# Tile-by-tile routing, folded queries on three bank pairs, sums by four heads, and a residual added by an identity product, in a two-layer perceiver kernel

## The reference

```python
    x = x + _L0_xattn_ref(_layernorm(x), ctx_1024, fside, ...)   # biased cross-attention and MLP
    x = x + _L0_attn_ref(_layernorm(x), ...)                     # linear memory with decay
    x = x + _L0_ffn_ref(_layernorm(x), ...)                      # 8 experts, all summed
    x = x + _L1_xattn_ref(_layernorm(x), ctx_1024, Wq, Wkv, Wout, bout)
    x = x + _L1_attn_ref(_layernorm(x), W_qkv, W_proj, b_proj, gamma, beta, ...)
    x = x + _L1_ffn_ref(_layernorm(x), Wr, br, 765.10:765.20 0.10, 0.10 (x1) 0.10 (x2) 0.10 (x1) 0.00 (x0) 0.00 (x0) 0.50 0.08 21, b1, 858.10:858.20 0.10, 0.00 (x0) 0.00 (x0) 0.00 (x0) 0.00 (x0) 0.00 (x0) 0.50 0.06 10, b2)

def _L1_xattn_ref(x, context, Wq, Wkv, Wout, bout):   # 16 heads of 64
    q, k, v = ...                                     # key j is seen by query i where j % 64 == i
    return softmax(mask(q @ k.T * 64 ** -0.5)) @ v @ Wout + bout

def _L1_attn_ref(x, W_qkv, W_proj, b_proj, gamma, beta, ...):   # 16 heads of 16
    attn = softmax(q @ k.T * 16 ** -0.5)
    return (attn @ v) @ W_proj.T + b_proj + layernorm(x, gamma, beta)

def _L1_ffn_ref(x, Wr, br, 765.10:765.20 0.10, 0.10 (x1) 0.10 (x2) 0.10 (x1) 0.00 (x0) 0.00 (x0) 0.50 0.08 21, b1, 858.10:858.20 0.10, 0.00 (x0) 0.00 (x0) 0.00 (x0) 0.00 (x0) 0.00 (x0) 0.50 0.06 10, b2):
    expert_idx = argmax(x @ Wr.T + br)                # one expert of 8 for each token
    y = relu(x @ 765.10:765.20 0.10, 0.10 (x1) 0.10 (x2) 0.10 (x1) 0.00 (x0) 0.00 (x0) 0.50 0.08 21[e].T + b1[e]) @ 858.10:858.20 0.10, 0.00 (x0) 0.00 (x0) 0.00 (x0) 0.00 (x0) 0.00 (x0) 0.50 0.06 10[e].T + b2[e]
    return y[expert_idx, token]
```

## Time and profile before

| | |
|---|---|
| median of three runs | 859.1 us (858.78 to 864.83) |
| profiled execution | 860.73 us, of it span 858.9 us |
| PE busy | 817.2 us, 95% of the span |
| DVE busy | 522.0 us, 61% |
| ACT busy | 417.3 us, 49% |
| POOL busy | 109.2 us, 13% |

### The profile page before, as it was taken

One profiled execution on the slowest core, in us unless ns is written; L12 is line 12 of the kernel. 1 busy time (PEld: TensorE's weight loads), 2 busy tenths in 40 slices (PEclk: granted clock), 3 DMA queues, 4 the chain that ended last, 5 costly groups with the idle time before them and its releaser, 6 DMA issues.

```text
span 858.9 us, 20559 instructions
## 1 busy us (share of the span) xinstructions
PE 817.2 (95%) x8272; PEld 670.2 (78%) x8272; DVE 522.0 (61%) x1231; ACT 417.3 (49%) x859; POOL 109.2 (13%) x96
## 2 busy tenths in 40 slices
PE   7999999999979798999999999999989999889997
PEld 5788888788756696888888888888668867668885
DVE  6778877788653756555555555775656632675422
ACT  4767666676652323555445544544356642532221
POOL 1333311340000050000000000520000000400100
PEclk9999999999999999999999999999999999999999
DMA  8446744576173000033033032300718607832960
GB/s 311 174 149 222 243 169 154 178 284 201 39 289 128 2 5 2 1 147 146 2 146 129 18 146 110 135 0 0 294 52 294 246 2 290 349 135 79 392 284 26
DMA packets 26020, 128.21 MB, mean 149 GB/s; under 512 B 2377, under 2 KB 8417, under 8 KB 21857
## 3 DMA queue, kind: packets, MB, share of 16 engines
q1 hardware_dynamic: 24624, 110.83, 34.6%
q0 software_dynamic: 1328, 16.41, 4.7%
HBM read 126.71 MB, written 0.52 MB: 148 GB/s over the span
## 4 chain that ended last, share of the span: by engine, by line
PE 82%; DVE 9%; DMA 4%; ACT 2%; issue 2%; SPq 1%; DVEq 0%
PE PS L471 14%; PE PS L472 14%; PE PS L473 14%; PE PS L779 5%; PE PS L1055 4%; PE PS L1240 3%; PE PS L900 3%; PE PS L1252 3%; PE PS L791 3%; PE PS L768 3%; DMA arena<-in_bias 3%; PE PS L491 2%; PE PS L1034 2%; PE PS L365 2%; PE PS L868 2%
## 5 line engine op out<-in xcount | busy, mean ns | idle before, releaser
L1789 DVE TENSOR_TENSOR w_l<-arena,w_h 128x768 fp32r<-128x768 f32 x64 | 65.5, 1025 | 81.4 <-ACT w_h L1425 81.3
L1425 ACT CAST w_h<-arena 128x768 fp32r<-128x768 f32 x64 | 53.4, 835 | 124.4 <-PE PS L473 124.4
L471 PE MATMUL PS<-xnT_h,w_h 128*128 128x512 f32 x256 | 99.8, 390 | 1.4 <-DVE xnT_l L465 1.4
L472 PE MATMUL PS<-xnT_l,w_h 128*128 128x512 f32 x256 | 99.7, 390 | 0.0
L473 PE MATMUL PS<-xnT_h,w_l 128*128 128x512 f32 x256 | 99.7, 389 | 0.0
L1629 DVE CUSTOM_DVE_ANT_0 arena<-PS,arena 128x512 f32<-128x512 f32 x128 | 86.8, 714 | 18.6 <-PE PS L768 17.0
L1319 ACT ACTIVATE arena<-arena 128x1024 f32<-128x1024 f32 x64 | 73.5, 1150 | 11.3 <-DVE arena L1629 11.2
L779 PE MATMUL PS<-consts,arena 128*128 128x128 f32 x512 | 68.3, 277 | 0.7 <-ACT arena L1324 0.4
L779 PEld LDWEIGHTS PS<-consts,arena 128*128 128x128 f32 x512 | 55.9, 141 | 10.5 <-issue 3.6
L1796 DVE TENSOR_TENSOR arena<-PS,arena 128x512 f32<-128x512 f32 x64 | 44.2, 690 | 27.6 <-PE PS L473 25.8
L471 PEld LDWEIGHTS PS<-xnT_h,w_h 128*128 128x128 f32 x256 | 48.1, 188 | 11.8 <-DVE xnT_l L465 1.8
(11 more groups left out here) (324 smaller groups left out, 1719.1 us busy)
## 6 DMA issues: line engine op xcount, KB each, us to landing
arena<-in_bias SPq DMA_DIRECT2D x64, 512.0 KB, 4.2
arena<-in_wall SPq DMA_DIRECT2D x8, 3072.0 KB, 10.1
arena<-in_wf SPq DMA_DIRECT2D x8, 2052.0 KB, 17.0
hT<-in_ctxT SPq DMA_DIRECT2D x8, 1024.0 KB, 5.7
arena<-in_ctxD SPq DMA_DIRECT2D x5, 1024.0 KB, 7.2
arena<-in_ctxG SPq DMA_DIRECT2D x5, 1024.0 KB, 4.9
hT<-in_ctxD SPq DMA_DIRECT2D x3, 1024.0 KB, 8.2
hT<-in_ctxG SPq DMA_DIRECT2D x3, 1024.0 KB, 4.8
```

Of the source, the lines that this page charges most:

```text
L471: pe.matmul(out, a[0], b[0], start=start, stop=False)
L472: pe.matmul(out, a[0], b[1], start=False, stop=False)
L1425: act.copy(w_h[:, s % 4, :], stage[s // 8 % 2][:, s % 8, :]).then_inc(sem("c_wh"), 1)
L1789: dve.tensor_tensor(w_l[:, s % 4, :], stage[s // 8 % 2][:, s % 8, :], wide(w_h[:, s % 4, :]), ALU.subtract).then_inc(sem("c_wl"), 1)
```

## The change

Five edits:

1. The folded queries use three pairs of neighbouring banks in turn instead of two fixed ones, by `folded_bank(c, dc)`. PE waits for the copies of three halves back. In the last chunk DVE and ACT share the four copies by h2 and not by half.
2. The sums of the heads are laid out four to a group of 32 partitions, by the new constants `sum0` and `sum1`, so that a tile's sums fill 128 columns of one bank. DVE takes the reciprocal of 128x128 (`inverse(t)`), PE spreads it back to all features by two products with the new constants `spread0` and `spread1` (`spread(t)`), ACT moves the weighted values out of PSUM (`values_out(t)`), DVE multiplies. The values alternate between two bank pairs.
3. The residual enters the projection as a product with the identity, ahead of the two products of the projection. Mean, variance and norm read PSUM; ACT copies the sum to `x_tok` afterwards.
4. Each tile's transposes go beside its projection in bank 4 + t, ACT copies both, and each tile's logits follow one tile behind. There are fewer fillers. The wait for `in_wrt` stands ahead of the first transposes.
5. The first token gather has two halves, by pairs of tiles of the table, and its two feature chunks lie in banks 0 and 1.

The core of the diff (of edit 5 the table's halves and the counters of later waits are left out):

```diff
+FIRST_OF, SECOND_OF = (1, 2, 4, 6), (3, 5, 7, 8)
...
+        parts[f"sum{kc}"] = (m // 16 == kc) & (m // 8 % 2 == p // 64)
+        parts[f"spread{kc}"] = p == 32 * (f // 32) + 16 * kc + 8 * (f // 16 % 2)
...
+    def folded_bank(c, dc):
+        return 2 + 2 * ((KC * c + dc) % 3)
...
-                    if c:
-                        pe.wait_ge(sem(f"d_ue{dc}"), 2 * c)
+                    if 2 * c + dc >= 3:
+                        before, half = divmod(2 * c + dc - 3, KC)
+                        pe.wait_ge(sem(f"d_ue{half}"), 2 * before + 2)
                     for n, (w, q) in enumerate(((wkT_h, qs_h), (wkT_h, qs_l), (wkT_l, qs_h))):
                         for h2, r in enumerate(halves):
-                            last = pe.matmul(bank(2 + 2 * h2 + dc), w[r, c, dc * P:(dc + 1) * P], q[r, c % 2, :],
+                            last = pe.matmul(bank(folded_bank(c, dc) + h2), w[r, c, dc * P:(dc + 1) * P], q[r, c % 2, :],
...
-                        pe.matmul(PS[32 * j:32 * j + 32, t, D + at(kc):D + at(kc) + P], C("pair32"),
-                                  PT[:, t, 2 * j + kc, :], start=True, stop=True)
+                        pe.matmul(PS[32 * j:32 * j + 32, 2 * (t % 2) + 1, 0:P], C(f"sum{kc}"),
+                                  PT[:, t, 2 * j + kc, :], start=kc == 0, stop=kc == KC - 1)
...
+            def spread(t):
+                pe.wait_ge(sem("e_a"), FIRST_OF[t])
+                pe.wait_ge(sem("e_te"), 6 if t < 2 else 10)
+                for kc in range(KC):
+                    last = pe.matmul(PS[:, 4 + t, D + kc * P:D + (kc + 1) * P], C(f"spread{kc}"), rie[:, t, :],
+                                     start=True, stop=True)
+                last.then_inc(sem("e_o"), 1)
+            def project(t):
+                pe.wait_ge(sem("e_yown"), 8)
+                pe.wait_ge(sem("e_a"), SECOND_OF[t])
+                pe.matmul(PS[:, 4 + t, 0:D], C("ident"), x_tok[:, t, :], start=True, stop=False)
+                for k in range(KC):
+                    last = pe.matmul(PS[:, 4 + t, 0:D], aT[:, k, t * P:(t + 1) * P],
+                                     wproj[:, k], start=False, stop=k == KC - 1)
+                last.then_inc(sem("e_out"), 1)
             for t in range(NT):
                 if t == 2:
                     turned(3)
-                pe.wait_ge(sem("e_te"), 2 * t + 2)
+                pe.wait_ge(sem("e_te"), (2, 4, 7, 10)[t])
+                if t >= 2:
+                    pe.wait_ge(sem("e_a"), FIRST_OF[t - 2])
                 weighted(t)
-            for t in range(NT):
-                pe.wait_ge(sem("e_a"), t + 1)
-                for k in range(KC):
-                    last = pe.matmul(PS[:, 4 + t, 0:D], aT[:, k, t * P:(t + 1) * P],
-                                     wproj[:, k], start=k == 0, stop=k == KC - 1)
-                last.then_inc(sem("e_out"), 1)
-            turn_tiles(pe, 9, xn_tok, 0, between=2)
-            warm(pe, 7, 1)
-            pe.wait_ge(sem("tr_sb"), 14)
-            pe.wait_ge(sem("in_wrt"), 32)
-            for t in range(NT):
+                if t:
+                    spread(t - 1)
+            project(0)
+            spread(3)
+            for t in range(1, NT):
+                project(t)
...
+            def turned_beside(t):
+                pe.wait_ge(sem("tr_src"), NT * 8 + t + 1)
+                for kc in range(KC):
+                    last = pe.transpose(PS[:, 4 + t, D + kc * P:D + (kc + 1) * P], xn_tok[:, t, kc * P:(kc + 1) * P],
+                                        C("ident"))
+                last.then_inc(sem("tr_ps"), 1)
+            def logits(t):
+                pe.wait_ge(sem("tr_sb"), 12 + t + 1)
                 for ki in range(KC):
                     last = pe.matmul(PS[:, 2, t * NEXP:(t + 1) * NEXP], xnT[:, ki, t * P:(t + 1) * P],
                                      wrt[:, ki, :], start=ki == 0, stop=ki == KC - 1)
-            last.then_inc(sem("f_log"), 1)
-            warm(pe, 7, 4)
+                return last
+            pe.wait_ge(sem("in_wrt"), 32)
+            for t in range(NT):
+                turned_beside(t)
+                if t:
+                    logits(t - 1)
+                if t < NT - 1:
+                    warm(pe, 3, 1)
+            logits(NT - 1).then_inc(sem("f_log"), 1)
+            warm(pe, 3, 3)
...
+            def first_gather():
+                for i in range(2):
+                    pe.wait_ge(sem("f_pick"), i + 1)
+                    for kc in range(KC):
+                        for t in (2 * i, 2 * i + 1):
+                            for part in (xn_h, xn_l):
+                                last = pe.matmul(PS[:, kc, 0:2 * P], part[:, t, kc * P:(kc + 1) * P], pick[0][:, t, :],
+                                                 start=t == 0 and part is xn_h, stop=t == NT - 1 and part is xn_l)
+                        if i:
+                            last.then_inc(sem("f_x"), 1)
...
+                for dc, h2 in ((1, 0), (1, 1)) if c + 1 < FC else ((0, 1), (1, 1)):
+                    act.wait_ge(sem(f"d_u{dc}"), 2 * c + h2 + 1)
+                    act.copy(U[dc][:, :, QI * (2 * c + h2):QI * (2 * c + h2 + 1)],
+                             bank(folded_bank(c, dc) + h2).rearrange("p (q i) -> p q i", i=QI)).then_inc(sem("d_ue1"), 1)
...
+            def values_out(t):
+                act.wait_ge(sem("e_o"), FIRST_OF[t])
+                act.copy(aT[:, :, t * P:(t + 1) * P],
+                         PS[:, 2 * (t % 2), 0:D].rearrange("p (k c) -> p k c", k=KC)).then_inc(sem("e_te"), 1)
+            values_out(0)
+            values_out(1)
             turned(3)
+            values_out(2)
+            values_out(3)
+            def turned_tile(t):
+                act.wait_ge(sem("tr_ps"), 16 + t + 1)
+                act.copy(xnT[:, :, t * P:(t + 1) * P],
+                         PS[:, 4 + t, D:2 * D].rearrange("p (k c) -> p k c", k=KC)).then_inc(sem("tr_sb"), 1)
+                act.copy(x_tok[:, t, :], PS[:, 4 + t, 0:D]).then_inc(sem("f_xnh"), 1)
             for t in range(NT):
                 tile_std(act, 9, t)
-            turned_act(act, 9, xnT, 0)
+                if t:
+                    turned_tile(t - 1)
+            turned_tile(NT - 1)
...
+                for dc, h2 in ((0, 0), (0, 1)) if c + 1 < FC else ((0, 0), (1, 0)):
+                    dve.wait_ge(sem(f"d_u{dc}"), 2 * c + h2 + 1)
+                    dve.tensor_copy(U[dc][:, :, QI * (2 * c + h2):QI * (2 * c + h2 + 1)],
...
+            def inverse(t):
+                dve.wait_ge(sem("e_o"), FIRST_OF[t])
+                dve.reciprocal(rie[:, t, :], PS[:, 2 * (t % 2) + 1, 0:P]).then_inc(sem("e_a"), 1)
             def output(t):
-                tk = slice(t * P, (t + 1) * P)
-                dve.wait_ge(sem("e_o"), t + 1)
-                num, total = (PS[:, t, i * D:(i + 1) * D].rearrange("p (k c) -> p k c", k=KC) for i in range(2))
-                ch.step(dve.reciprocal(rie[:, :, tk], total))
-                dve.tensor_tensor(aT[:, :, tk], num, rie[:, :, tk], ALU.mult).then_inc(sem("e_a"), 1)
+                dve.wait_ge(sem("e_o"), SECOND_OF[t])
+                dve.wait_ge(sem("e_te"), (7, 8, 11, 12)[t])
+                num, inv = aT[:, :, t * P:(t + 1) * P], PS[:, 4 + t, D:2 * D].rearrange("p (k c) -> p k c", k=KC)
+                dve.tensor_tensor(num, num, inv, ALU.mult).then_inc(sem("e_a"), 1)
             for t in range(NT):
                 scores(t)
+            inverse(0)
             for t in range(NT):
+                if t + 1 < NT:
+                    inverse(t + 1)
                 output(t)
+            def summed(t):
+                return PS[:, 4 + t, 0:D]
+            def normed(t):
+                tile_inverse(dve, ch, 9, t)
+                dve.tensor_scalar(xn_tok[:, t, :], summed(t), mv[:, t, 0:1], rstd[:, t:t + 1], ALU.subtract, ALU.mult)\
+                   .then_inc(sem("tr_src"), 1)
             dve.wait_ge(sem("e_yown"), 8)
-            residual_norm(dve, ch, 9, sem("e_out"), (4, 5, 6, 7), x_tok, x_tok, xn_tok)
+            for t in range(NT):
+                dve.wait_ge(sem("e_out"), t + 1)
+                ch.step(dve.bn_stats(stats[:, t, :], summed(t)))
+                dve.bn_aggr(mv[:, t, :], stats[:, t, :]).then_inc(sem("ln_var"), 1)
+                if t:
+                    normed(t - 1)
+            normed(NT - 1)
```

39 lines of the change are left out of this document (19 added, 20 removed).

## The result

The kernel became slower, not faster: 865.4 us, median of 20 executions (858.65 to 868.79), beside 860.15 for the kernel before (858.77 to 864.83, 20 executions). The ratio is 1.0044, 95% interval 1.0031 to 1.0058. Forecast were 856.7 us and a range of 854.0 to 860.5; the forecast started from 859.1 us for the kernel before, the median of three executions, so 1.05 us of the distance of 8.7 us lies in that starting point. The profiled execution took 867.34 us around a span of 865.5, against 860.73 around 858.9.

The account below looks back on a forecast made before the run. TensorE was busy 95% of the span, but the three changed places were taken as serial chains. Gains of 1.1 (folded queries), 0.56 (self-attention and routing) and 0.7 (gather), 2.4 us, off 859.1 gave 856.7 us; range 854.0 to 860.5.

Parts of the forecast that it names:

- Folded queries: Last step's first half no longer waits for DVE's copies; similarity products start at 639.78 instead of 640.89, gain 1.1 us.
- Self-attention's output: Shorter DVE reciprocals, 3.4 us added PE work; PE becomes the bound, projection result at 765.2 against 763.62, 1.6 us slower.
- rival (c): Added products in self-attention don't overlap, each paying a 0.26 us tail, 3.1 us more: 859.8 us; chance 0.08.
- The wait for the router's weights: First router transposes now wait for the weights' DMA, landing 1.95 us after issue; PE starts them at 767.25.
- the count from the second issue: Reading of the router weights' DMA cost by which the landing would be 0.4 us later.
- Rival (b): Router's weights aren't late or their wait is hidden under the norm; chain ends 2.2 us sooner, 854.5; chance 0.12.
- the chain behind the wait: Router transposes to first DVE routing step take 4.8 us, at 772.05 instead of 772.61; parts 2 and 3 gain 0.56.
- The gather: First token gather starts after half the choice table, at 777.4 instead of 778.10, gain 0.7 us.
- If it falls again for as long: In the new wait, a low clock lasting the earlier 3.4 us adds up to 1.7 us, about 1.3.
- Rival (a): PE's clock falls in the new wait before the router transposes, adding about 1.3 us: 858.0 us; chance 0.33.
- From here PE is busy to the end and moves as a block: From the first gather on, PE's work keeps its length and only shifts; weight loads keep their distance.
- the landing at its upper bound: Router weights land 3.3 us after their issue instead of 1.95, delaying the first router transposes.

Follow-up runs that it names:

- the filled kernel: Changed kernel with five more filler products ahead of the wait for the router's weights; 860.73 us, ratio 1.0001 to the kernel before.
- after: The changed kernel itself, all five edits against the kernel before; 865.4 us, ratio 1.0044.
- the gap put back: Changed kernel with early router weights and 512-column fillers, its expert-bias wait moved ahead of the first router transposes; 858.86 us, ratio 0.9992.
- the wide fillers: Changed kernel, wait kept, with 512-column products for pairs of 256 in the second and sixth turn, 12 passes fewer; 860.23 us, ratio 1.0013.
- the old filler counts: Changed kernel with the filler numbers of the kernel before, the wait for the router's weights kept; 863.08 us, ratio 1.0025.
- after, the second time: The changed kernel measured again, unchanged, on the chip of two other kernels; 866.50 us, ratio 1.0063.
- fillers cut in two: Kernel before with sixth-turn fillers as four of 128 columns for two of 256, 12 passes more; 864.67 us, ratio 1.0036.
- only the queries: Kernel before with only the folded queries' three bank pairs and shared last copies; 860.87 us, ratio 0.9987.

## Why the prediction was wrong, point by point

**Folded queries: right.** 639.8 was forecast, 639.61 came, and 1.04 us with this part alone. What was not seen is that 0.6 of it goes again at the stop 7 us later.

**Self-attention's output: right.** The reciprocal takes 0.96 us (0.94 forecast), PE is the bound, and from the first spread to the end of the last projection it is 10.5 us in the filled kernel and 10.6 in after, for 10.4. The added products issue back to back, so rival (c) has fallen. After reaches the first spread late because the clock was down at 752 to 756: pass by pass it is level with the filled kernel at 752 (0.03 us) and 1.37 us behind it at 756, and its first transposes come 1.35 us later (767.93 and 766.58).

**The wait for the router's weights: right.** The transposes start 1.95 us after the first issue, for 2.01 forecast, and 1.53 after the second (766.40), so the count from the second issue, which put the landing 0.4 us later, was wrong here. Rival (b) has fallen. Undisturbed the chain behind the wait is 4.78 us for 4.8.

**The gather: right** up to its start, 4.81 us behind the first routing step for 4.79.

**"If it falls again for as long": the step that failed.** Rival (a) named the mechanism, with a chance of 0.33 and a price of 1.3 us, from the 3.4 us at the lower level in the earlier trace rows. A long fall came in 17 of 26 executions of the changed kernel, lasted 14 us in the trace, and cost 5.7 us there (4.8, 5.4 and 5.7 between the executions of one kernel with and without it, for the gap put back, after and the wide fillers). The fault was to take the length of one fall, ahead of a chain with two fillers between tiles, for the length of any, while the same change thinned that chain and put more idle time in one piece ahead of it. The text even cited, for this rival, the rule of the Trainium skill that activity releases the low clock (TensorE: Matmul & The Clock Gate, What's actually happening); here PE's rows read 2.00 busy of 2.00 and the clock stayed down. With the fall priced at its size rival (a) stands at 856.7 + 5.7 = 862.4 us and not at 858.0, outside the range; the stop of 1.5 us below and the 1.05 us of the starting point bring that to 864.9, beside 865.4 measured. The upper end of the range was short by its own terms as well: rival (c) at 859.8 and the landing at its upper bound of 3.3 us for 1.95 add up to 861.2, not to 860.5.

**"From here PE is busy to the end and moves as a block": failed too**, by 1.5 us. A block of PE work does not move unchanged when the number of instructions ahead of it changes: here the stop of 1.21 us in the experts' group came with 8284 passes for 8272. The prediction had no term for it.

The four losses of the first table follow: 1.35 + 0.43 ahead of the transposes (clock; the filled kernel is 0.43 behind the forecast there as well), 2.0 and 3.7 behind them (clock), 1.5 from the gather to the end (stop): 9.0. Without the long fall the change gives at most 1.2 us of the forecast 2.4 (the seven executions of after, 860.7 beside 860.15; wait filled, ratio 1.0001; wide fillers, 859.9 beside 861.1); with the wait taken away as well, 2.4 to 3.9 (ratios 0.9972 to 0.9955).

## What to carry over

In this kernel a wait that stood free ahead of a chain of small PE steps had two prices: its own length, and in many executions a clock at half speed through the whole chain, so price the fall over the chain behind it and not over the gap, and load early what is a few KB. When PE runs long groups of very small products, count its instructions: a dozen more or fewer anywhere ahead can make or hide a stop of one to two microseconds that the profile puts down to "issue".

## What the runs showed of the hardware

- The lower clock lasted 14 us in after and some 17 us with the old filler counts, with PE busy in every stretch. Every other fall in the traces ahead of the final output DMA lasted some 3.4 us, but for one of 7 us in the first 16 us of the kernel with the shortened start. Most of them lie near 11, 294 and 748 us; others near 134 us (after, the second time), 649 us (fillers cut in two) and 765 us (before and only the queries).
- PE stopped for 0.3 to 2.33 us, mostly at the same three places of its program (5586, 6591 and some 7604 passes from its start), and went on 1.26 to 1.56 us after a 16 KB packet of the instruction queue had ended, in 43 of 43 such stops. So these stops are the arrival of PE's instructions.
- A filler pass of 256 columns costs 0.23 us at full clock in a row of 22 (5.00 us); a row of six takes 1.54 us at full clock and 2.91 us at the lower level.
- With the idle products at the very start shortened, PE was 2.5 us behind the trace of before at 47 us and 1.5 us behind from 200 us on.
